# A decoder layer as one program instead of four, with each stage begun inside the end of the one in front

## What is computed

```python
x = _layernorm(x + _L0_attn_ref(x, w_qkv, b_qkv, w_out, b_out))         # 32 heads of 16, ALiBi, causal
x = _layernorm(x + _L0_xattn_ref(x, ctx, ctx, mask, wq, wk, wv, wo, 0)) # 32 query heads, 8 kv heads, 128 wide, RoPE
x = _layernorm(x + _L0_ffn_ref(x, gate_w, up_w, down_w, fc1_w, fc2_w, expert_w, ln_gamma, ln_beta))
```

## Time and profile before

| | us |
|---|---|
| median of 3 runs | 995.8 (995.36 to 997.18) |
| the profiled execution, its own time | 994.21 |
| span of its trace | 992.3 |
| PE busy | 922.1 (93%) |
| DVE busy | 697.4 (70%) |
| ACT busy | 500.0 (50%) |
| POOL busy | 467.1 (47%) |

### The profile page before, as it was taken

The page is one execution under the profiler, slowest core; times in us unless marked ns, Lnnn a source line. Parts: engine busy times, 40 slices in busy tenths (PEclk is TensorE's granted clock), DMA queues, the critical chain, the costliest instruction groups (busy, mean ns, idle before and its releaser), DMA issues. The chain is left out here.

```text
span 992.3 us, 15681 instructions
## 1 busy us (share of the span) xinstructions
PE 922.1 (93%) x4812; PEld 776.6 (78%) x4812; DVE 697.4 (70%) x2195; ACT 500.0 (50%) x1565; POOL 467.1 (47%) x390
## 2 busy tenths in 40 slices
PE   7975999999998678999999999999999997799996
PEld 6754888888886557888888888888888885588885
DVE  5355688777777556777777777777777778674646
ACT  5233988777774225545545544554554555251220
POOL 4465543222222556666666566666666645321101
PEclk9977899999998978999999999999999999899998
DMA  7666577566662611112031211313112102200000
GB/s 265 231 250 130 149 196 183 133 129 149 138 182 86 243 32 33 33 52 108 33 125 35 100 51 43 118 33 127 33 32 107 35 20 85 95 13 22 22 7 37
DMA packets 68386, 96.63 MB, mean 97 GB/s; under 512 B 6096, under 2 KB 43216, under 8 KB 67152
## 3 DMA queue, kind: packets, MB, share of 16 engines
q1 hardware_dynamic: 68304, 95.64, 32.4%
HBM read 68.33 MB, written 27.26 MB: 96 GB/s over the span
## 5 line engine op out<-in xcount | busy, mean ns | idle before, releaser
L929 ACT ACTIVATE C_qh<-C_t 128x512 fp32r<-128x512 f32 x64 | 40.5, 633 | 181.3 <-POOL C_t L1128 181.3
L34 PE MATMUL C_pj<-xTh,wh 128*128 128x512 f32 x256 | 102.3, 399 | 6.2 <-DVE xTl L128 5.9
L34 PE MATMUL C_yb<-woh,C_oh 128*128 128x512 f32 x256 | 104.3, 408 | 3.1 <-DVE C_ol L1098 2.2
L1132 POOL TENSOR_TENSOR C_ql<-C_t,C_qh 128x512 fp32r<-128x512 f32 x64 | 82.7, 1292 | 47.6 <-ACT C_qh L929 47.6
L670 ACT ACTIVATE B_prob<-B_prob,B_top 128x128 f32<-128x128 f32 x256 | 99.0, 390 | 7.3 <-DVE B_top L774 7.3
L34 PE MATMUL C_pj<-xTl,wh 128*128 128x512 f32 x256 | 101.8, 398 | 0.0
L34 PE MATMUL C_pj<-xTh,wl 128*128 128x512 f32 x256 | 101.7, 397 | 0.0
L34 PE MATMUL C_yb<-woh,C_ol 128*128 128x512 f32 x256 | 101.6, 397 | 0.0
L34 PE MATMUL C_yb<-wol,C_oh 128*128 128x512 f32 x256 | 101.6, 397 | 0.0
L950 ACT ACTIVATE C_prob<-C_prob,C_top 128x128 f32<-128x128 f32 x256 | 99.0, 391 | 0.0
L1128 POOL TENSOR_TENSOR C_t<-C_t 128x512 f32<-128x512 f32 x64 | 83.0, 1297 | 18.4 <-DVE C_t L1058 18.4
(11 more groups left out here) (237 smaller groups left out, 2739.3 us busy)
## 6 DMA issues: line engine op xcount, KB each, us to landing
kv<-cross_kv_d SPq DMA_DIRECT2D x8, 2048.0 KB, 8.4
cross_kv_d<-B_k_out SPq DMA_DIRECT2D x16, 512.0 KB, 3.3
cross_kv_d<-B_v_out SPq DMA_DIRECT2D x16, 512.0 KB, 4.5
stage<-wq_dram SPq DMA_DIRECT2D x32, 256.0 KB, 2.7
stage<-wo_dram SPq DMA_DIRECT2D x32, 256.0 KB, 2.9
heads_q_d<-cTl SPq DMA_DIRECT2D x16, 256.0 KB
heads_k_d<-cTl SPq DMA_DIRECT2D x16, 256.0 KB
heads_q<-heads_q_d SPq DMA_DIRECT2D x32, 128.0 KB, 3.9
```

Of the source, the lines that this page charges most:

```text
L34: mm = eng.matmul(out, stationary[i], moving[j], start=first and n == 0, stop=last and n == len(PASSES) - 1)
L1132: eng.tensor_tensor(query(r, 1), by_batch(t1[:, r % 2, :]), query(r, 0).bitcast(F32), ALU.subtract).then_inc(s_qlo, 1)
```

## The change

The four blocks become one (`decoder_layer` opens one `nc.Block()`); the stages are classes (`ProjectSelf`, `AttendSelf`, `AttendCross`, `FeedForward`) with one method for each engine, and the loop over steps calls the methods of two stages in turn. All SBUF and PSUM buffers get fixed places (`Chip`), so that those of one stage can lie where those of the stage in front are dead. The single rings for weights become one ring for B, C and D.

- **A into B.** The last three v tiles (`LATE = 3`) are made in steps 0 to 2 of B, after that step's scores. x is loaded in eight transfers of 256 KB in steps 0 to 7 of B and not in A; POOL adds the bias in steps 6 to 13. The key and value products start at step 3 (`OFF = 3`, was 2) and go through two banks in another order (k, k, v, v).
- **In B.** Layer norm (`Rows`) is by batch: statistics 8 steps after a batch's closing began, then the root on POOL, `normalise` one step later, four transposes on PE two steps later, hi and lo three steps later. Before, this was done for four batches at a time at the borders.
- **B into C.** B has 12 steps to drain. In them the first cross-attention weights are split (`NEXT_SPLIT`) and the first four query products made (`QUERY` at steps 66, 67, 69, 71) and rotated (`ROTATE`). `project(4)`, which stood ahead of C's step 0, stands in it, behind the scores.
- **C into D.** From step 58 on the feed-forward weights are split, two pieces a step, all subtractions on POOL; statistics of batch n-59, normalise of n-60, transposes of n-61 and hi/lo of n-62 follow in each step. Both `lat` products are made in steps 60 and 61 and the first two `up` products in steps 65 and 66. The subtractions of the `down` weights go from DVE to POOL.
- **Layout.** The turned x is stored batch by batch (`[P, B, 2, C, S]`), so that the moving operand of 1008 matmuls (768 of `C_pj`, 240 of up and fc1) is four runs of 128 floats and no longer one of 512.

The matmuls and their shapes are the same ones; none is added or removed.

```diff
-        xT = [sb("xT" + s, [P, C, NT], F32R) for s in ("h", "l")]
...
+        xT = chip.at("xT", Chip.VALUES, [P, B, 2, C, S], F32R)
...
+        block = ctx.enter_context(nc.Block())
...
+        @block.tensor
+        def _(eng):
+            a.tensor(eng)
+            for n in range(b.STEPS):
+                b.tensor(eng, n)
+            for n in range(c.STEPS):
+                d.tensor_ahead(eng, n)
+                c.transpose(eng, n)
+                c.scores(eng, n)
+                c.outputs(eng, n)
+                d.tensor_between(eng, n)
+                c.values(eng, n)
+                c.queries(eng, n)
+                d.tensor_behind(eng, n)
+            d.tensor(eng)
...
-                if i == C:
-                    eng.dma_start(x1[:, :, :], x_d).then_inc(s_x, 16)
...
+            if n < B:
+                eng.dma_start(self.x1[:, n, :], self.dram["x_nat"][:, n, :]).then_inc(self.s_x[n], 16)
...
+    NEXT_LOAD = {57: range(5), 62: (5, 6), 69: (7, 8), 71: (9,), 72: (10,)}
+    NEXT_SPLIT = {60: 0, 61: 1, 67: 2, 68: 3, 69: 4, 70: 5, 71: 6, 72: 7}
+    QUERY = {66: 0, 67: 1, 69: 2, 71: 3}
+    ROTATE = {67: 0, 68: 1, 70: 2, 72: 3}
...
+    SPLIT = {58: (0, 1), 59: (2, 3), 60: (4, 5), 61: (6, 7), 62: (8, 9), 63: (10, 11), 64: (12,)}
+    DOWN = 13
+    STATS, NORMAL, TURN, TAKE = 59, 60, 61, 62
+    LAT = (60, 61)
+    FIRST = 65
...
+    def statistics(self, eng, b):
+
+        eng.bn_stats(self.stats[:, b, :], self.x[:, b, :]).then_inc(self.s_stats, 1)
+        eng.wait_ge(self.s_stats, b + 1)
+        eng.bn_aggr(self.moments[:, b, :], self.stats[:, b, :]).then_inc(self.s_moments, 1)
+        eng.wait_ge(self.s_moments, b + 1)
+        var = self.moments[:, b, 1:2]
+        eng.tensor_scalar(var, var, EPS, None, ALU.add).then_inc(self.s_var, 1)
```

More of the change, by code:

```diff
@@ L57, in inverse_root, with wait @@
[L57 to L73 removed]
+def wait(eng, sem, value):
+    if value > 0:
+        eng.wait_ge(sem, value)
```

2379 lines of the change are left out of this document (1208 added, 1171 removed).

## The result

The changed kernel takes 1012.9 us (1008.7 to 1014.8, four runs), the kernel before 995.6 (993.9 to 997.2): a ratio of 1.017 (1.015 to 1.020). It is 1.7% slower. The forecast was 967, range 950 to 984; both the direction and the range were wrong. The profiled execution took 1012.7 us, its span 1010.9.

The account below looks back on a forecast made before the run. PE bounds the dense stretches; 83.8 us of its losses hang on five places. Span 992.3 − 6 − 0 + 2 − 14.2 − 10.4 = 963.7, plus 1.9 outside it and 1.6 to the median: forecast 967 us, range 950 to 984.

Parts of the forecast that it names:

- Inside A, 6 us less: Without x's load in A, the wait for a store shrinks and the v weights come sooner; loss 10.3 becomes 4.3 us.
- A to B: Border of A and B: no change, 16.1 us lost as before, from 8.9 + 6.8 + 0.4.
- the 0.4 behind it: After B's steps 0 to 2: 0.4 us lost before the first key product, for v bias and first key weight.
- In B, 2 us more: B's dense steps: layer norm adds 17 us to DVE over seven batches, PE stays the bound, 2 us more lost.
- I take 0.3 per batch: In B, PE's wait at the next transposes after each closing: 0.3 us per batch, bounds 0 and 2.
- B to C, 13.3: From B's last outputs to C's first scores: POOL's queue decides, 25 us long, PE loses 13.3 where 27.4 before.
- POOL is without a gap: Sign that the forecast is right: POOL works without a gap before C's first scores.
- C to D, 11: Late C to D: DVE's steps of 7.4 to 7.7 us exceed PE's 5.2; loss 21.4 becomes 11 us.
- of waiting for POOL's root: Late C steps: 0.8 us of DVE waiting for POOL's root, counted in DVE's step of 7.4 to 7.7 us.
- The split moving operand: The moving operand of 1008 matmuls as four runs of 128 floats: taken to cost 0, at most 0.03 us each.
- The rival with 997: Rival: the split operand costs PE 0.03 us per matmul, 30 us over 1008 matmuls, 997 us; chance 0.05.
- The rival "DVE becomes the bound": Rival: DVE bounds B at each closing, 2 us per batch, and C's end at 8.5 a step; 983 us; chance 0.15.

Follow-up runs that it names:

- late statistics: Changed kernel with one edit: in B, DVE makes a batch's statistics behind the rotation's copies, not ahead of them; 999.2 us, 1.006.
- x in A: Changed kernel with x loaded in A again as one 2 MB transfer, none in B; 1017.2 us, 1.023.
- eight edits: Changed kernel with the five edits, all v tiles ahead of B, second small product two steps behind the first, D's roots made when asked; 967.3 us, 0.974.
- four and five edits: Changed kernel: POOL's root first, B's statistics later, ACT's turned-rows copy and C's first exponentials earlier, 981.1 us; fifth, late C's normalisation at step end, 976.8 us.
- the new drain: On top of eight edits, order in B's drain and C's first steps changed: query copies later, fourth rotation behind the last normalisation; 968.5 us, 0.974.
- the spread additions: On top of eight edits, POOL's eight bias additions spread over steps 10 to 37 of B; 968.4 us, 0.974.

## Why the prediction was wrong

- **Inside A, 6 us less: right within 1 us.** 5.1 by undoing it. A's own loss is 9.4 where 8.1 was forecast, since the last split of the v weights came at 58.0 and not near 56.
- **A to B.** The wait for the heads was forecast at 8.9 and measured 8.98, the loop of three steps 16.8 and 16.6. The step that failed is the 0.4 behind it: the clock stayed at half (0.50) to 107.8, for the 9.3 us from the first key product on, which cost some 4, and the next value weight's split cost 1.3. The text had this as "3 more", as a possibility, and should have had it in the sum, as the clock of the earlier trace rows was 0.59 in that stretch.
- **In B, 2 us more: the step that failed first.** It was 18. "I take 0.3 per batch", with 0 and 2 as bounds, came from DVE's load of 5.1 us against PE's 2.9 in one step and a mean of 85%. What decides is where in DVE's list the two things stand that PE waits for: the statistics ahead of the copy that frees a bank, and a wait of DVE for ACT in the midst of the step. Each cost 1.1 us a batch, 13 waits and 14.6 us in all, at the bound of 2 per batch that was kept for the range alone; the fall of the clock behind one of them added 3.2. (One of the 13 is the product of 1.48 that DVE and POOL contend for, below.) With the two moved, and all the work still there, B loses 8.1 where the forecast for it was 6.6.
- **B to C, 13.3: right for the border itself, wrong for what reached into it.** The 13.3 was counted from B's last outputs. From there (345.61) C's first scores come after 24.7 us, forecast 25, with 12.8 lost; the table's 20.3 begins at B's last scores and has 7.5 more, lost ahead of the last outputs. The sign "POOL is without a gap" wasn't met: from the first sum (347.47) to the last split POOL takes 22.8 us and idles 5.3 of them, 3.0 for ACT's copies, which the forecast's sum holds, and 2.3 for DVE's rotations. The 6 us above belong to the same order on DVE: a wait of 2.45 at 331.89 for the rotation's copy, and the low clock after it (0.81, 0.50 and 0.66 in the stretches of 5 us from 330). Most of it is the clock: with ACT's copy moved instead the wait of 2.45 stayed, no fall followed, and 5 us went. Moving the statistics took the loss to 14.2. C's first steps lost 10.8 for 8.5.
- **C to D, 11: the step that failed is the 0.8 "of waiting for POOL's root".** It was 2.9 to 3.5 in each of five steps, for POOL's queue had two pieces ahead of the root, and these wait for ACT. The diff's order showed it: `gpsimd_between` issues the pieces first. The 1.1 for a normalisation was 0.55 here, and became 1.50 when the root came in time. With root and normalisation moved the border loses 13.2; the wait for the first small product, forecast 3.2, was 3.42.
- **The split moving operand: right.** A query product of C's middle has 12 matmuls in 2.73 us, 0.2275 each, and a C step is 7.51 to 7.53 as before. The rival with 997 had the right side of the result by the wrong mechanism.
- **The rival "DVE becomes the bound"** named the mechanism of C's end ("a wait of DVE for POOL's root stops everything queued behind it") and dismissed it with POOL's load of 27%. In B's middle it was another wait: DVE never waits for a root there, but 1.32 us for ACT's copy in six batches. Its chance of 0.15 and its price of 16 us were both too small: waits in each batch of B, and those at C's end, cost some 30. The forecast of "faster" at 0.93 took the two as if they couldn't happen together.
- **D, forecast at 1.0 to 1.2, lost 3.3.** Left out altogether: POOL's roots stand behind all eight additions of beta (911.84 to 922.3 in the rows below), DVE waits 1.75 for the first, and PE then 1.29 at 926.13, with a clock of 0.71 in the 5 us from 925. With roots and additions in turn the wait is 0.24 and D loses 1.7.

```profile
911.84 10.47 POOL L1553 TENSOR_TENSOR x<-x,D_beta 128x512 f32<-128x512 f32 x8
922.27 0.55 POOL L1556 TENSOR_TENSOR D_rstd<-D_moments,power 128x1 f32<-128x1 f32 x1
```

What stays open: which of the many waits of about 1.1 us is followed by a low clock, and why runs of one kernel spread over up to 12 us.

## What to carry to other kernels

When work is moved into a loop that another engine paces, don't compare loads: go through each engine's list of that step, and ask of each instruction that the pacing engine waits for what now stands ahead of it, and on whom that waits. A busy share of 77 or 27% says nothing on it; the edits that made 1.7% slower into 1.4% faster changed no instruction, only four places in the lists of three engines. And put an operation that everybody's step hangs on (a root of 0.55 us) at the head of its queue, and its use as late as the data allow.

## What the runs showed of the hardware

**Two operands in SBUF.** Beyond what was expected of it (the normalisations of the earlier trace rows had 1.90 and 4.78), a DVE product could be held up for four POOL operations in a row. One of 0.42 us took 0.81 to 0.84 in every second closing of the changed kernel, beside one subtraction on POOL, 1.48 in its step 12 (which is PE's wait of 1.06 at 134.55) and 5.16 to 5.17 in the traces of three others: late statistics, x in A, eight edits. POOL's operations there, from the kernel with eight edits, with the DVE product:

```profile
127.75 1.28 POOL L166 TENSOR_TENSOR B_wout<-stage,B_wout 128x512 fp32r<-128x512 f32 x1
128.98 3.70 POOL L610 TENSOR_TENSOR x<-x,B_bout 128x512 f32<-128x512 f32 x3
...
127.81 5.16 DVE L813 TENSOR_TENSOR B_o<-B_o,B_rden 128x256 f32<-128x256 f32 x1
```

In the changed kernel the product starts just as long after the same subtraction, and POOL has no gap either, but there it got in behind that one operation:

```profile
132.25 1.28 POOL L166 TENSOR_TENSOR B_wout<-stage,B_wout 128x512 fp32r<-128x512 f32 x1
133.48 1.46 POOL L610 TENSOR_TENSOR x<-x,B_bout 128x512 f32<-128x512 f32 x1
...
132.32 1.48 DVE L813 TENSOR_TENSOR B_o<-B_o,B_rden 128x256 f32<-128x256 f32 x1
```

It ended 0.3 us behind the subtraction and not with POOL's run, as an expectation above has it, and POOL's next addition took 1.46 where the ones after it take 1.3. What decides between one operation and four isn't shown.

**TensorE's clock.** A fall to 1.2 GHz came behind a wait of no more than 1.1 us, though not behind each. The changed kernel around 240 us, behind the wait of 1.11 that ends at 240.18 (clock: third number from the right):

```profile
235.00:240.00 5.00, 4.07 (x30) 3.56 (x29) 4.85 (x17) 3.21 (x11) 2.37 (x3) 1.00 0.27 107
240.00:245.00 5.00, 4.82 (x20) 4.40 (x21) 3.70 (x22) 2.17 (x9) 2.56 (x2) 0.60 0.00 0
245.00:250.00 5.00, 5.00 (x27) 4.48 (x26) 1.62 (x10) 2.76 (x11) 0.00 (x0) 0.72 0.64 218
```

PE was busy all the while, and the two steps took 10.9 us where the same two of other batches took 7.7: 3.2 us for one fall. The 12 other waits of this size in B's middle had none behind them. In the traces, B's middle has one to four falls in each kernel that has such waits all along (four in the one with late statistics, whose runs spread most, and four in the one with x in A). It has none in the kernel before and in those with four and five edits, with the new drain and with the spread additions, which have one wait of at most 1.07 there; in the one with eight edits it has one, which begins within the wait of 4.76. So a short wait repeated in a dense loop can cost more than its length. That it also makes runs differ isn't shown: the runs of the kernels with four and five edits, whose traces have no fall there, spread over 10 us as well.
